# Cross attention with keys on the partitions: two heads a slot, no transposes of probabilities, values as one plain fp32 matmul

## The chip, the cores and the metric

One core of a Trainium2 chip runs the whole program. The metric is device time in microseconds, and the median of three runs is compared.

## The reference

One perceiver layer on x (256 tokens x 1024) with a context of 4096 tokens. Three sublayers, each behind a layer norm and added to x: cross attention, a decayed linear attention, and a mixture of low-rank experts. The change is in the first:

```python
q = (latents @ Wq).reshape(b, q_len, 4, 8, 128)           # 32 query heads, 4 key heads
k = (hidden_states @ Wk).reshape(b, kv_len, 4, 128)       # context and latents: 4352 rows
v = (hidden_states @ Wv).reshape(b, kv_len, 4, 128)
scores = jnp.einsum('bqhgd,bkhd->bhgqk', q, k) / sqrt(128)
attn = jax.nn.softmax(scores, axis=-1)
out = jnp.einsum('bhgqk,bkhd->bqhgd', attn, v)
return out.reshape(b, q_len, 4096) @ Wo
```

## The kernel before, in words

The program is a row of blocks, one after the other: keys and values (`project_keys_values`), attention (`cross_attention`), its output projection, the linear attention, its projection, the mixture. In each block the five engines run hand-written instruction lists, ordered by semaphores. SyncE (SP) issues all DMAs.

Precision: a matrix that goes through TensorE is split into a high part (rounded to fp32r, the format of TensorE's one-pass mode) and the rest, low. `three_pass` (L105 to L107) makes a product of three matmuls: high by high, high by low, low by high. Transposes run on plain fp32.

**Keys and values.** The context comes in eight chunks of 512 rows and one of the 256 latent rows. ScalarE copies the keys out of PSUM (`copy_keys`), VectorE the values, and both are stored in DRAM; the keys go there unsplit. The attention loads a key head in pieces and splits it again: ScalarE the high part (`act_piece`, L606), GpSimd the low (`pool_piece`, L682).

**Attention.** A slot serves one head; 32 slots, eight for each key head. Queries are on the partitions: scores of 128 queries x 512 keys, 18 units for a head (`pe_scores`), copied out by VectorE with the scale and a running maximum (`dve_scores`, L722). ScalarE exponentiates whole rows and sums them on the way (`act_exp`, L620). Probabilities are then transposed, two key tiles at a time, by TensorE (`pe_turn`, L822: four transposes of 128 x 128), split by ScalarE (L626) and VectorE (L747), and multiplied with the split values in three matmuls of 256 columns a key tile (`pe_values`). A step j of the slot does this for one pair of the 34 key tiles, so 17 steps; the scores of the next head, the query of the head after that (`pe_query`: 24 matmuls of 256 columns) and the inverse sums (`dve_inverse`, a diagonal spread by a matmul with ones, L853 and L854) are placed between. VectorE scales the output (L756) and SP stores it (L553).

Of the kernel before, what the change touches and what calls it, by code (L numbers as in the profile page):

```python
# [31 lines left out]
P = 128  # L32
# [52 lines left out]
class Shared:  # L85
# [3 lines left out]
    def __init__(self, a):  # L89
        self.r = [a.sb(f"split{i}", [P, KV], F32R) for i in range(2)]  # L90
        self.f = a.sb("full", [P, KV])
        self.stage = a.sb("stage", [P, 2 * PIECE])
        self.out = a.sb("head_out", [P, 2, TOK])


        self.last_keys = carve(self.f, 0, KVH, TOK)
        self.k_stored = a.sem("k_stored")
        self.v_stored = a.sem("v_stored")
        self.first_keys = [region[:, 0:FIRST * PIECE] for region in self.r]
        self.first_weight = [carve(region, FIRST * PIECE, KT, D) for region in self.r]  # L100
# [91 lines left out]
def project_keys_values(nc, x, ctxT, wk, wv, wq, x_sb, hT_hi, hT_lo, ident, kT_dram, v_dram, shared):  # L192
# [5 lines left out]
    with ExitStack() as ctx:  # L198
# [9 lines left out]
        k_out = a.sb("k_out", [P, KVH, CCHUNK])  # L208
# [17 lines left out]
        v_ready = a.sem("v_ready")  # L226
        k_copied = a.sem("k_copied")
# [4 lines left out]
        first_raw = (carve(shared.f, 0, KT, D), shared.f[:, KT * D:KT * D + FIRST * PIECE])  # L232
        first_split = list(zip(shared.first_weight, shared.first_keys))
# [8 lines left out]
        def store(sp, c, tiles, k_out):  # L242

            n = tiles * P
            sp.wait_ge(k_copied, KVH + KVH * (c + 1))
            sp.dma_start(kT_dram[:, :, bass.ds(c * CCHUNK, n)].rearrange("g p n -> p g n"),
                         k_out[:, :, 0:n]).then_inc(k_stored, 16)
            sp.wait_ge(v_copied, VT * (c + 1) + tiles)
            sp.dma_start(v_dram[:, :, bass.ds(c * VT, tiles), :].rearrange("g p t d -> p g t d"),
                         v_out[:, :, 0:tiles, :]).then_inc(v_stored, 16)  # L250

        @block.sync
        def _(sp):
            sp.sem_inc(k_stored, 16)
# [9 lines left out]
            sp.dma_start(x_sb[:, :, :], x).then_inc(x_in, 16)  # L264
            with sp.Fori(0, NCHUNK - 2) as c:
                sp.wait_ge(c_lo_ready, c + 1)
                load(sp, c + 2)
                store(sp, c, VT, k_out)
            store(sp, NCHUNK - 2, VT, k_out)
            sp.wait_ge(c_lo_ready, NCHUNK - 1)  # L270
            sp.dma_start(first_raw[0], wq[0]).then_inc(first_in, 16)
            sp.wait_ge(first_in, 16)
            sp.wait_ge(k_stored, 16 * NCHUNK)
            sp.dma_start(first_raw[1], kT_dram[0, :, 0:FIRST * PIECE]).then_inc(first_in, 16)
            store(sp, NCHUNK - 1, VT, k_out)
            store(sp, NCHUNK, QT, shared.last_keys)

        def copy_keys(act, c, n, k_out=k_out):

            for g in range(KVH):  # L280
                act.wait_ge(k_ready, KVH * c + g + 1)
                act.activation(k_out[:, g, 0:n], k_ps[:, g, 0:n], ACT.Copy).then_inc(k_copied, 1)
# [8 lines left out]
        def _(act):  # L291
            act.sem_inc(k_copied, KVH)
# [12 lines left out]
            with act.Fori(0, NCHUNK // 2 - 1) as i:  # L305
                for par in range(2):
                    c = 2 * i + 1 + par
                    next_hi(act, c, par)
                    act.wait_ge(k_stored, 16 * (c + 1))
                    copy_keys(act, c, CCHUNK)  # L310
            act.wait_ge(k_stored, 16 * NCHUNK)
# [3 lines left out]
            for i in range(2):  # L315
                act.wait_ge(first_in, 16 * (i + 1))
                act.activation(first_split[0][i], first_raw[i], ACT.Copy).then_inc(first_hi_ready, 1)
            act.wait_ge(first_lo_ready, 2)
            copy_keys(act, NCHUNK, TOK, shared.last_keys)

        @block.gpsimd
        def _(pool):
            for i in range(2):
                pool.wait_ge(first_hi_ready, i + 1)
                pool.tensor_tensor(first_split[1][i], first_raw[i], f32(first_split[0][i]),
                                   ALU.subtract).then_inc(first_lo_ready, 1)
# [14 lines left out]
        def _(dve):  # L341
            dve.sem_inc(v_copied, VT)
            for k in range(KT):
# [7 lines left out]
            split_low(dve, 1, 1)  # L351
            dve.wait_ge(x_in, 16)
# [7 lines left out]
            with dve.Fori(0, NCHUNK // 2 - 1) as i:  # L360
                for par in range(2):
                    c = 2 * i + 1 + par
                    split_low(dve, c + 1, par)
                    copy_values(dve, c, VT)
            ln.dve_lo(dve)
            copy_values(dve, NCHUNK - 1, VT)
# [23 lines left out]
        def _(pe):  # L390
# [22 lines left out]
            for t in range(QT):  # L413
# [7 lines left out]
PAIRS = KVT // 2  # L421
UNITS = [(qt, c0, min(BANK, KV - c0)) for qt in range(QT) for c0 in range(0, KV, BANK)]
NU = len(UNITS)
UPR = NU // QT
NS = 4
NPT = 3
LAG = 2
S_LAST = 11
DOUBLE = NU - 1 - S_LAST
UNITS_OF_STEP = [range(2 * j, 2 * j + 2) if j < DOUBLE else range(j + DOUBLE, j + DOUBLE + 1) if j <= S_LAST  # L430
                 else range(0) for j in range(PAIRS)]
Q_STEPS = range(S_LAST + 1, PAIRS - 1)


def piece_of(end):

    return (end - 1) // PIECE


def cross_attention(nc, wq, kT_dram, v_dram, hT_hi, hT_lo, ident, oT_dram, shared, proj):  # L440
# [9 lines left out]
    with ExitStack() as ctx:  # L450
        a = Alloc(nc, ctx, "xa_")
        v_hi = a.sb("v_hi", [P, KV], F32R)
        v_lo = a.sb("v_lo", [P, KV], F32R)
        kT_hi, kT_lo = shared.r
        rows = [[shared.f if (i, t) == (0, 0) else a.sb(f"rows{i}{t}", [P, KV]) for t in range(QT)] for i in range(2)]
        stage = [shared.stage[:, i * PIECE:(i + 1) * PIECE] for i in range(2)]
        w_raw = a.sb("w_raw", [P, KT, D])
        w_hi = a.sb("w_hi", [P, KT, D], F32R)
        w_lo = a.sb("w_lo", [P, KT, D], F32R)
        qT_hi = a.sb("qT_hi", [P, TOK], F32R)  # L460
        qT_lo = a.sb("qT_lo", [P, TOK], F32R)
        pT_hi = [a.sb(f"pT_hi{i}", [P, 2, TOK], F32R) for i in range(NPT)]
        pT_lo = [a.sb(f"pT_lo{i}", [P, 2, TOK], F32R) for i in range(NPT)]
        maxima = a.sb("maxima", [P, 2, QT, UPR])
        neg_max = a.sb("neg_max", [P, 2, QT])
        sums = a.sb("sums", [P, 2, QT, PIECES])
        total = a.sb("total", [P, QT])
        inverse = a.sb("inverse", [P, QT])
        ones = a.sb("ones", [P, P], F32R)
        diag_hi = a.sb("diag_hi", [P, TOK], F32R)  # L470
        diag_lo = a.sb("diag_lo", [P, TOK], F32R)
        scale_rows = a.sb("scale_rows", [P, TOK])
        o_out = [shared.out[:, i, :] for i in range(2)]
        s_ps = a.ps("s_ps", [P, NS, BANK])
        t_ps = a.ps("t_ps", [P, 2, 2, TOK])
        o_ps = a.ps("o_ps", [P, 2, TOK])
        m_ps = a.ps("m_ps", [P, 2, TOK])


        piece_asked = a.sem("piece_asked")  # L480
        piece_in = [a.sem(f"piece_in{i}") for i in range(2)]
        piece_hi = a.sem("piece_hi")
        piece_lo = a.sem("piece_lo")
# [3 lines left out]
        q_ready = a.sem("q_ready")  # L487
        q_hi_ready = a.sem("q_hi_ready")
        q_lo_ready = a.sem("q_lo_ready")
        s_ready = a.sem("s_ready")  # L490
        s_drained = a.sem("s_drained")
        max_ready = a.sem("max_ready")
        exp_done = a.sem("exp_done")
        turned = a.sem("turned")
        pT_hi_ready = a.sem("pT_hi_ready")
        pT_lo_ready = a.sem("pT_lo_ready")
        pv_done = a.sem("pv_done")
        sum_ready = a.sem("sum_ready")
        ones_set = a.sem("ones_set")
        diag_ready = a.sem("diag_ready")  # L500
        spread = a.sem("spread")
        spread_copied = a.sem("spread_copied")
        o_ready = a.sem("o_ready")
        o_stored = proj.stored
        block = ctx.enter_context(nc.Block())

        def slots(eng, kv_head_slot):

            def kv_head(g, last):
                for u in range(2):
                    kv_head_slot(eng, g, GROUP * g + u, u, last)
                with eng.Fori(1, GROUP // 2 - 1) as i:
                    for par in range(2):
                        kv_head_slot(eng, g, GROUP * g + 2 * i + par, 2 + par, last)
                for u in range(GROUP - 2, GROUP):
                    kv_head_slot(eng, g, GROUP * g + u, u, last)

            with eng.Fori(0, KVH - 1) as g:  # L520
                kv_head(g, False)
            kv_head(KVH - 1, True)

        def flags(u, last):

            return not (last and u == GROUP - 1), not (last and u >= GROUP - 2)

        def ahead(n, par, j):

            return (n, par, j + LAG) if j + LAG < PAIRS else (n + 1, 1 - par, j + LAG - PAIRS)  # L530

        def pt_free(n, j):

# [1154 lines left out]
```

## Time and profile before

| | |
|---|---|
| median of 3 runs | 2156.7 us (2156.37 to 2159.44) |
| profiled execution: its time, its span | 2159.04 us, 2157.2 us |
| TensorE matmuls, weight loads | 98%, 90% of the span |
| VectorE, ScalarE, GpSimd | 58%, 50%, 9% |
| DMA | mean 92 GB/s, 199.28 MB |
| granted TensorE clock | 0.994 |

Shares are busy time over the span. A busy TensorE isn't one at its peak, since its matmuls overlap and their ends are modelled; distances between starts say what one costs. In the rows PE is TensorE, PEld its weight loads, DVE VectorE, ACT ScalarE, POOL GpSimd, SP SyncE; L105 is line 105 of the kernel. Names that begin with xa_ are the attention's, kv_ the keys stage's, wo_ and lo_ the projections', la_ and pair_ the linear attention's; `full`, `split` and `stage` are buffers that the stages share.

### The profile page before, as it was taken

What the parts mean: (1) busy time and instruction counts of PE and PEld (TensorE: products, weight loads), DVE (VectorE), ACT (ScalarE), POOL (GpSimd) and SP (SyncE); (2) the same over time, 40 slices, a digit from 0 to 9 for tenths busy, and PEclk for the clock granted to TensorE, in tenths of its full rate; (3) what the DMA queues carried; (4) which work ended last, traced back from release to release, by engine and by line L of the source; (5) the groups of instructions that cost most, each with busy time, mean ns of one, the idle gap of its engine ahead of it and who ended that gap; (6) DMA issues with size and microseconds to landing.
All of it is one profiled execution on the core that took longest, in us unless ns stands there. A gap on an engine that the chain in (4) does not pass through costs nothing. (4 is left out here: it accounts for less than half of the span.)

```text
span 2157.2 us, 38230 instructions
## 1 busy us (share of the span) xinstructions
PE 2111.0 (98%) x14054; PEld 1937.6 (90%) x14054; DVE 1247.2 (58%) x2591; ACT 1070.2 (50%) x1604; POOL 192.2 (9%) x98
## 2 busy tenths in 40 slices
PE   8999999999999999999999999999999999999998
PEld 6888888799998999998999899998779999999886
DVE  5211110567676767766676767676574566666555
ACT  4111111566566656575666666566444544455442
POOL 0000001300012100031000310000000000000110
PEclk9999999999999999999999999999999999999999
DMA  6222212200012000120000210001745444455362
GB/s 234 102 113 97 78 69 80 82 26 13 24 45 78 14 26 12 46 75 27 14 25 30 76 41 13 26 12 55 274 148 209 181 175 175 179 189 191 133 233 79
DMA packets 57385, 199.28 MB, mean 92 GB/s; under 512 B 4592, under 2 KB 22000, under 8 KB 51760
## 3 DMA queue, kind: packets, MB, share of 16 engines
q1 hardware_dynamic: 57264, 197.71, 25.7%
q8 instruction: 71, 1.16, 0.2%
q14 instruction: 50, 0.41, 0.1%
HBM read 170.43 MB, written 27.26 MB: 92 GB/s over the span
## 5 line engine op out<-in xcount | busy, mean ns | idle before, releaser
L747 DVE TENSOR_TENSOR xa_pT_lo<-xa_t_ps,xa_pT_hi 128x512 fp32r<-128x512 f32 x544 | 372.6, 690 | 334.9 <-ACT xa_pT_hi L626 334.7
L626 ACT ACTIVATE xa_pT_hi<-xa_t_ps 128x512 fp32r<-128x512 f32 x544 | 321.8, 597 | 411.9 <-PE xa_t_ps L822 400.9
L105 PE MATMUL xa_o_ps<-xa_pT_hi,xa_v_hi 128*128 128x256 f32 x1088 | 310.1, 285 | 2.2 <-DVE xa_pT_lo L747 2.1
L107 PE MATMUL xa_o_ps<-xa_pT_hi,xa_v_lo 128*128 128x256 f32 x1088 | 308.5, 284 | 0.0
L106 PE MATMUL xa_o_ps<-xa_pT_lo,xa_v_hi 128*128 128x256 f32 x1088 | 307.9, 283 | 0.0
L822 PE MATMUL xa_t_ps<-ident,xa_rows 128*128 128x128 f32 x1632 | 294.8, 273 | 2.9 <-DVE xa_pT_lo L747 2.9
L722 DVE TENSOR_SCALAR_CACHE_REDUCE xa_rows<-xa_s_ps 128x512 f32<-128x512 f32 (+1 forms) x432 | 274.7, 652 | 0.2 <-PE xa_s_ps L107 0.2
L105 PE MATMUL xa_s_ps<-split,xa_qT_hi 128*128 128x512 f32 (+1 forms) x576 | 250.9, 436 | 0.9 <-DVE xa_qT_lo L716 0.9
L620 ACT ACTIVATE xa_rows<-xa_rows,xa_neg_max 128x1088 f32<-128x1088 f32 x192 | 229.6, 1196 | 0.0
L105 PEld LDWEIGHTS xa_o_ps<-xa_pT_hi,xa_v_hi 128*128 128x128 f32 x1088 | 207.2, 190 | 16.8 <-DVE xa_pT_lo L747 3.4
L107 PE MATMUL xa_s_ps<-split,xa_qT_lo 128*128 128x512 f32 (+1 forms) x576 | 220.8, 383 | 0.0
L106 PEld LDWEIGHTS xa_o_ps<-xa_pT_lo,xa_v_hi 128*128 128x128 f32 x1088 | 207.1, 190 | 13.8
L106 PE MATMUL xa_s_ps<-split,xa_qT_hi 128*128 128x512 f32 (+1 forms) x576 | 219.4, 381 | 0.0
L107 PEld LDWEIGHTS xa_o_ps<-xa_pT_hi,xa_v_lo 128*128 128x128 f32 x1088 | 207.4, 191 | 0.0
L822 PEld LDWEIGHTS xa_t_ps<-ident,xa_rows 128*128 128x128 f32 x1632 | 202.4, 141 | 4.0 <-issue 3.6
L1300 DVE TENSOR_TENSOR pair_lo<-pair_raw,pair_hi 128x4096 fp32r<-128x4096 f32 x30 | 132.8, 4425 | 81.2 <-ACT pair_hi L1237 81.2
L333 DVE COPY stage<-kv_v_ps 128x512 f32<-128x512 f32 x34 | 23.5, 691 | 243.2 <-PE kv_v_ps L107 243.2
L105 PE MATMUL la_qk_ps<-hT_hi,pair_hi 128*128 128x256 f32 x512 | 145.7, 285 | 2.8 <-PEq L928 2.8
L686 POOL TENSOR_TENSOR xa_w_lo<-xa_w_raw,xa_w_hi 128x1024 fp32r<-128x1024 f32 x31 | 74.5, 2403 | 798.4 <-ACT xa_w_hi L611 798.4
L107 PE MATMUL la_qk_ps<-hT_hi,pair_lo 128*128 128x256 f32 x512 | 145.6, 284 | 0.0
L106 PE MATMUL la_qk_ps<-hT_lo,pair_hi 128*128 128x256 f32 x512 | 145.6, 284 | 0.0
L822 PE MATMUL xa_t_ps<-ident,full 128*128 128x128 f32 x544 | 133.4, 274 | 6.1 <-DVE xa_pT_lo L747 6.1
(287 smaller groups left out, 4744.8 us busy)
## 6 DMA issues: line engine op xcount, KB each, us to landing
pair_raw<-in_w_qk SPq DMA_DIRECT2D x15, 2048.0 KB, 8.3
pair_raw<-in_w_gv SPq DMA_DIRECT2D x15, 2048.0 KB, 8.3
full<-in_wo SPq DMA_DIRECT2D x16, 1024.0 KB, 5.2
pair_raw<-in_w_out SPq DMA_DIRECT2D x16, 1024.0 KB, 5.1
xa_w_raw<-in_wq SPq DMA_DIRECT2D x31, 512.0 KB, 3.7
full<-in_ctxT SPq DMA_DIRECT2D x7, 2048.0 KB, 8.3
stage<-v_scratch SPq DMA_DIRECT2D x16, 544.0 KB, 3.8
kT_scratch<-kv_k_out SPq DMA_DIRECT2D x8, 1024.0 KB, 4.1
```

What stands on the lines that cost most here:

```text
L105: pe.matmul(out, w_hi, m_hi, start=first, stop=False)
L106: pe.matmul(out, w_hi, m_lo, start=False, stop=False)
L107: return pe.matmul(out, w_lo, m_hi, start=False, stop=last)
L333: dve.tensor_copy(v_out[:, :, t, :], v_ps[:, t, :].rearrange("p (g d) -> p g d", d=D)).then_inc(v_copied, 1)
L620: act.activation(row, row, ACT.Exp, bias=neg_max[:, par, qt:qt + 1], accum_out=sums[:, par, qt, e:e + 1]).then_inc(exp_done, 1)
L626: act.activation(pT_hi[j % NPT][:, :, :], t_ps[:, (par * PAIRS + j) % 2, :, :], ACT.Copy).then_inc(pT_hi_ready, 1)
L686: pool.tensor_tensor(w_lo[:, :, :], w_raw[:, :, :], f32(w_hi[:, :, :]), ALU.subtract).then_inc(w_lo_ready, 1)
L722: dve.tensor_scalar(rows[par][qt][:, c0:c0 + width], s_ps[:, (par * NU + k) % NS, 0:width], SCALE, None, ALU.mult, ALU.max, accum_out=maxi ...
L747: dve.tensor_tensor(pT_lo[j % NPT][:, :, :], t_ps[:, (par * PAIRS + j) % 2, :, :], f32(pT_hi[j % NPT][:, :, :]), ALU.subtract).then_inc(pT ...
L822: last = pe.transpose(t_ps[:, (par * PAIRS + j) % 2, t, qt * P:(qt + 1) * P], rows[par][qt][:, at], ident[:, :])
L1300: dve.tensor_tensor(w_lo[part][:, :, :], raw[part][:, :, :], f32(w_hi[part][:, :, :]), ALU.subtract).then_inc(w_lo_ready[part], 1)
```

## The change

- A slot serves two heads that share a key head: 16 slots. Keys are on the partitions, and both heads' queries (512) are the moving columns: a step j scores two key tiles into two banks of PSUM (`pe_scores`), and there are two such buffers.
- VectorE keeps an element-wise maximum over all key tiles (`dve_peak`) and ScalarE copies the scores out (`act_row`). At the slot's end the maximum is turned by four transposes (`pe_peak`), reduced (`dve_max`), put on a diagonal (`act_diag`) and spread over the partitions by a plain fp32 matmul with ones (`pe_spread`). In the next slot VectorE subtracts it (`dve_shift`) and ScalarE exponentiates (`act_exp`), step by step.
- The probabilities lie as the value matmul needs them: no transposes of them, no split. `pe_values` is one plain fp32 matmul of 512 columns a key tile.
- The sums are added by GpSimd (`pool_add`), spread by ones (`pe_sums`), inverted by four reciprocals of 128 columns (`dve_inverse`); ScalarE copies the output out (`act_output`), GpSimd scales it (`pool_output`). In the last slot VectorE takes half of the adds.
- Keys are split once, in the keys stage (ScalarE high, VectorE low: `copy_low_keys`), and stored in two parts, eight DMAs a chunk; values are stored whole. The attention loads both into place, in four pieces (`ENDS`), without another split. The query weight of two heads is loaded and split at once (2048 columns), and pe_query has 48 matmuls.

```diff
-                for qt in range(QT):
-                    last = pe.transpose(t_ps[:, (par * PAIRS + j) % 2, t, qt * P:(qt + 1) * P],
-                                        rows[par][qt][:, at], ident[:, :])
-            last.then_inc(turned, 1)
...
+        def pe_spread(pe, n, first=False):
+            pe.wait_ge(diag_ready, (W // P) * (n + 1))
+            if not first:
+                pe.wait_ge(shifted, J * n)
+            pe.matmul(r_ps[:, :], ones[:, :], diag[:, :], start=True, stop=True).then_inc(spread, 1)
...
+            pe.wait_ge(exp_done, J * n + j + 1)
             for t in range(2):
                 at = slice((2 * j + t) * P, (2 * j + t + 1) * P)
-                last = three_pass(pe, o_ps[:, par, :], v_hi[:, at], v_lo[:, at], pT_hi[j % NPT][:, t, :],
-                                  pT_lo[j % NPT][:, t, :], j == 0 and t == 0, j == PAIRS - 1 and t == 1)
+                last = pe.matmul(o_ps[:, :], v[:, at], probs[j % KEEP][:, t, :], start=j == 0 and t == 0,
+                                 stop=j == J - 1 and t == 1)
             last.then_inc(pv_done, 1)
...
+        def pe_slot(pe, n, u, g, first=False, last=False):
+            has_prev, has_next, has_query = flags(u, first, last)
+            par = u % 2
+            keys = g + 1 if u == 3 else None
+            values = g if u == 0 else None
+            if has_next:
+                pe_scores(pe, n + 1, 1 - par, (u + 1) % 2, 0, keys)
+            for j in range(J):
+                if has_next and j + 1 < J:
+                    pe_scores(pe, n + 1, 1 - par, (u + j) % 2, j + 1, keys)
+                pe_values(pe, n, j, values, not has_prev)
+                if has_prev and j == 2:
+                    pe_sums(pe, n - 1)
+            if has_next:
+                pe_peak(pe, n + 1)
+                if has_query:
+                    pe_query(pe, n + 3, 0, FILL)
+                pe_spread(pe, n + 1)
+                if has_query:
+                    pe_query(pe, n + 3, FILL, 2 * KT)
...
+        def pe_scores(pe, n, par, b, j, keys, first=False):
...
+            if not first or j >= 2:
+                pe.wait_ge(row_ready, J * n + j - 1)
             for t in range(2):
                 at = slice((2 * j + t) * P, (2 * j + t + 1) * P)
+                last = three_pass(pe, s_ps[:, 2 * b + t, :], kT_hi[:, at], kT_lo[:, at], qT_hi[:, par, :], qT_lo[:, par, :],
+                                  True, True)
+            last.then_inc(s_done, 1)
...
+        def act_row(act, n, b, j, first=False):
+            act.wait_ge(peak_done, J * n + j + 1)
+            if not first:
+                act.wait_ge(exp_done, J * (n - 1) + j + 1)
+            act.activation(rows[j], s_ps[:, 2 * b:2 * b + 2, :], ACT.Copy).then_inc(row_ready, 1)
...
+            for j in range(J):
+                if j + 1 < J:
+                    act_exp(act, n, j + 1, not has_prev, not has_next)
+                if has_next:
+                    act_row(act, n + 1, (u + 1 + j) % 2, j)
+                if has_next and has_query and j == 2:
+                    act_query(act, n + 2, u % 2)
...
+                if has_query and j == 4:
+                    act_weight(act, n + 3)
...
+            if j < J - 2:
+                dve.tensor_tensor(peak[:, :, :], s_ps[:, 2 * b:2 * b + 2, :], peak[:, :, :], ALU.max).then_inc(peak_done, 1)
+                if j == J - 3:
+                    dve.wait_ge(peak_done, J * n + j + 1)
+                    dve.tensor_tensor(peak[:, 0, :], peak[:, 0, :], peak[:, 1, :], ALU.max).then_inc(peak_part, 1)
+                return
...
+        def dve_shift(dve, n, j):
+            dve.wait_ge(row_ready, J * n + j + 1)
+            dve.wait_ge(spread, n + 1)
+            dve.tensor_tensor(rows[j], rows[j], r_ps[:, :].unsqueeze(1).to_broadcast([P, 2, W]), ALU.subtract).then_inc(shifted, 1)
...
+            for j in range(J):
                 if has_next:
+                    dve_peak(dve, n + 1, (u + 1 + j) % 2, j)
+                if j + 1 < J:
+                    dve_shift(dve, n, j + 1)
...
+                if has_prev and 4 <= j < 8:
+                    dve_inverse(dve, n - 1, j - 4)
...
+                pool.wait_ge(added, (J - 1) * n + j - 1)
+                pool.tensor_tensor(sums[:, :, :], sums[:, :, :], probs[j % KEEP], ALU.add).then_inc(added, 1)
...
+            for g in range(KVH):
+                dve.wait_ge(k_hi_ready, KVH * c + g + 1)
+                dve.tensor_tensor(k_lo[:, g % 2, 0:n], k_ps[:, g, 0:n], f32(k_hi[:, g % 2, 0:n]),
+                                  ALU.subtract).then_inc(k_copied, 1)
```

`W` is 512, `J` 17, `KEEP` 3 (probability buffers), `FILL` 12, `PAIRS` 16 now counts pairs of heads. `flags` gives has_prev (not the first slot), has_next (not the last) and has_query (not the last three); GpSimd's `pool_slot` does an add a step, the weight's low part at j = 6 and `pool_output` at j = 9.

## Rows read from the trace of the kernel before

**Rows 1.** Windows: stretch, its length, then busy us (count) of each engine, clock, DMA share, GB/s.
```profile
0.00:385.40 385.40, 375.16 (x1696) 312.34 (x1696) 78.26 (x89) 68.79 (x77) 10.68 (x10) 1.00 0.30 108
385.40:1519.60 1134.20, 1116.55 (x8000) 1044.46 (x8001) 783.95 (x2019) 704.76 (x1185) 147.87 (x60) 0.99 0.11 36
```

**Rows 2.** Waits in the attention stage: engine, waiting tile <- releaser: total us, times, longest.
```profile
ACT xa_pT_hi L626 <- PE xa_t_ps L822: 400.9, 341, 2.7
...
PE xa_t_ps L822 <- DVE xa_pT_lo L747: 9.0, 7, 2.0
```

**Rows 3.** Timeline of TensorE, transposes and value matmuls: start us, us, instruction.
```profile
902.88 0.27 PE L822 MATMUL xa_t_ps<-ident,full 128*128 128x128 f32 x1
902.99 0.27 PE L822 MATMUL xa_t_ps<-ident,xa_rows 128*128 128x128 f32 x1
...
904.82 0.28 PE L106 MATMUL xa_o_ps<-xa_pT_lo,xa_v_hi 128*128 128x256 f32 x1
904.94 0.28 PE L107 MATMUL xa_o_ps<-xa_pT_hi,xa_v_lo 128*128 128x256 f32 x1
```

**Rows 4.** Timeline, handing over between engines, and two VectorE operations in a row.
```profile
390.52 0.42 DVE L716 TENSOR_TENSOR xa_qT_lo<-xa_m_ps,xa_qT_hi 128x256 fp32r<-128x256 f32 x1 [6.37 <-ACT xa_qT_hi L615]
391.00 0.50 PE L105 MATMUL xa_s_ps<-split,xa_qT_hi 128*128 128x512 f32 x1 [0.93 <-DVE xa_qT_lo L716]
...
391.57 0.39 PE L107 MATMUL xa_s_ps<-split,xa_qT_lo 128*128 128x512 f32 x1
391.80 0.40 PE L105 MATMUL xa_s_ps<-split,xa_qT_hi 128*128 128x512 f32 x1
...
392.10 0.69 DVE L722 TENSOR_SCALAR_CACHE_REDUCE full<-xa_s_ps 128x512 f32<-128x512 f32 x1 [1.16 <-PE xa_s_ps L107]
...
901.25 1.29 DVE L747 TENSOR_TENSOR xa_pT_lo<-xa_t_ps,xa_pT_hi 128x512 fp32r<-128x512 f32 x2 [0.53 <-ACT xa_pT_hi L626]
```

**Rows 5.** Timeline of SP's queue: the output stores of two consecutive heads.
```profile
831.80 0.35 SPq L553 DMA_DIRECT2D oT_scratch<-head_out  x1
...
866.34 0.35 SPq L553 DMA_DIRECT2D oT_scratch<-head_out  x1
```

**Rows 6.** Line 1059, four plain fp32 matmuls of one column: ns min/median/max, first, last start.
```profile
L1059 PEld LDWEIGHTS lo_turned<-ones,square_sum x8: 187/192/195, 2036.8 to 2037.6; 128*128 128x128 f32 x8
L1059 PE MATMUL lo_turned<-ones,square_sum x8: 242/250/253, 2036.8 to 2037.6; 128*128 128x1 f32 x8
```

**Rows 7.** Groups by form: busy us, mean ns of one | idle before it.
```profile
L747 DVE TENSOR_TENSOR xa_pT_lo<-xa_t_ps,xa_pT_hi 128x512 fp32r<-128x512 f32 x544 | 372.6, 690 | 334.9 <-ACT xa_pT_hi L626 334.7
L626 ACT ACTIVATE xa_pT_hi<-xa_t_ps 128x512 fp32r<-128x512 f32 x544 | 321.8, 597 | 411.9 <-PE xa_t_ps L822 400.9
...
L620 ACT ACTIVATE xa_rows<-xa_rows,xa_neg_max 128x1088 f32<-128x1088 f32 x192 | 229.6, 1196 | 0.0
...
L1300 DVE TENSOR_TENSOR pair_lo<-pair_raw,pair_hi 128x4096 fp32r<-128x4096 f32 x30 | 132.8, 4425 | 81.2 <-ACT pair_hi L1237 81.2
...
L1237 ACT ACTIVATE pair_hi<-pair_raw 128x4096 fp32r<-128x4096 f32 x30 | 108.2, 3608 | 0.0
...
L611 ACT ACTIVATE xa_w_hi<-xa_w_raw 128x1024 fp32r<-128x1024 f32 x31 | 32.6, 1050 | 0.1
```

**Rows 8.** Groups by form: VectorE's reciprocals of two columns and of one.
```profile
L734 DVE RECIPROCAL xa_inverse<-xa_total 128x2 f32<-128x2 f32 x32 | 5.3, 166 | 1.1
...
L153 DVE RECIPROCAL lo_ln_r<-lo_ln_root 128x1 f32<-128x1 f32 x2 | 0.3, 154 | 0.3 <-ACT lo_ln_root L169 0.3
```

**Rows 9.** Line 686, GpSimd's subtraction of 1024 columns: ns min/median/max.
```profile
L686 POOL TENSOR_TENSOR xa_w_lo<-xa_w_raw,xa_w_hi x31: 2394/2406/2408, 395.0 to 1440.5; 128x1024 fp32r<-128x1024 f32 x31
```

**Rows 10.** Timeline of TensorE after a wait near the stage's start.
```profile
408.67 0.33 PE L822 MATMUL xa_t_ps<-ident,full 128*128 128x128 f32 x1 [1.99 <-DVE xa_pT_lo L747]
...
410.08 0.63 PE L105 MATMUL xa_s_ps<-split,xa_qT_hi 128*128 128x512 f32 x1
410.50 0.63 PE L106 MATMUL xa_s_ps<-split,xa_qT_hi 128*128 128x512 f32 x1
```

More of the change, by code:

```diff
@@ L253, in _ @@
         def _(sp):
-            sp.sem_inc(k_stored, 16)
+            for par in range(2):
+                sp.sem_inc(k_stored[par], 32)
             sp.sem_inc(v_stored, 16)
@@ L440, in cross_attention, with piece_of, starts_piece @@
-def cross_attention(nc, wq, kT_dram, v_dram, hT_hi, hT_lo, ident, oT_dram, shared, proj):
+FILL = 12
+KEEP = 3
+def piece_of(j):
+    return next(i for i, end in enumerate(ENDS) if j < end)
+def starts_piece(j):
+    return j == 0 or j in ENDS
+def cross_attention(nc, wq, k_drams, v_dram, hT_hi, hT_lo, ident, ones, oT_dram, shared, proj):
     with ExitStack() as ctx:
         a = Alloc(nc, ctx, "xa_")
-        v_hi = a.sb("v_hi", [P, KV], F32R)
-        v_lo = a.sb("v_lo", [P, KV], F32R)
         kT_hi, kT_lo = shared.r
[L455 to L483, printed above, removed]
@@ new lines, in act_exp @@
+        def act_exp(act, n, j, first=False, last=False):
+            act.wait_ge(shifted, J * n + j + 1)
+            back = j - KEEP
+            if back >= 0:
+                act.wait_ge(pv_done, J * n + back + 1)
+                if not last:
+                    act.wait_ge(added, (J - 1) * n + max(back, 1))
+                elif back >= 2 and back % 2 == 0:
+                    act.wait_ge(added_last, back // 2)
+                else:
+                    act.wait_ge(added, (J - 1) * n + (back + 2) // 2)
+            elif not first:
+                before = max(x for x in range(J) if x % KEEP == j)
+                act.wait_ge(pv_done, J * (n - 1) + before + 1)
+                act.wait_ge(added, (J - 1) * (n - 1) + before)
+            act.activation(probs[j % KEEP], rows[j], ACT.Exp, scale=SCALE).then_inc(exp_done, 1)
@@ new lines, in pe_sums, with pe_sums_last @@
+        def pe_sums(pe, n):
+            pe.wait_ge(sum_ready, n + 1)
+            pe.wait_ge(max_ready, n + 2)
+            pe.matmul(t_ps[:, :], ones[:, :], sum_row[:, :], start=True, stop=True).then_inc(sum_spread, 1)
+        def pe_sums_last(pe):
+            pe.wait_ge(inverse_ready, 4 * LAST + 4)
+            pe.wait_ge(added, (J - 1) * LAST + J // 2)
+            pe.wait_ge(added_last, J // 2)
+            pieces = [part[:, t, :] for part in (sums, peak) for t in range(2)]
+            for i, part in enumerate(pieces):
+                last = pe.matmul(t_ps[:, :], ones[:, :], part, start=i == 0, stop=i == len(pieces) - 1)
+            last.then_inc(sum_spread, 1)
```

710 lines of the change are left out of this document (343 added, 367 removed).

## The prediction

> **What bounds the kernel now.** I read the windows by stage first, then who waited for whom in the attention stage, then TensorE's timeline inside it. The attention stage lies from 385.4 to 1519.6 us: 1134.2 us, 53% of the span, and TensorE is busy in 1116.6 of them, VectorE in 784, ScalarE in 705, GpSimd in 148 [rows 1]. TensorE's longest waits there are below 10 us a line; the large ones are those of ScalarE and VectorE for TensorE's transposes [rows 2]. So the stage costs what TensorE's instructions cost back to back. Busy times overstate that, since matmuls overlap, so I take distances between starts: a transpose of 128 columns every 0.11 us, a value matmul of 256 every 0.12 [rows 3], a score matmul of 512 every 0.23 [rows 4]. One head by these prices: scores 3 x (16 x 0.23 + 2 x 0.12) = 11.8, values 34 x 3 x 0.12 = 12.2, transposes 68 x 0.11 = 7.5, query 24 x 0.12 = 2.9, spreading the inverse sums 0.2: 34.6 us. The stores of two consecutive heads are 34.54 us apart [rows 5]. The price list holds; a pair of heads costs 69.2.
>
> **TensorE after the change.** One slot now serves two heads. Scores: 34 key tiles x 3 x 0.23, that is 1.38 a step of two tiles. The 136 transposes (15.0) go; four of the maximum (0.44) come. Query as before, 48 x 0.12 = 5.8. Values: one plain fp32 matmul of 512 columns for each key tile, in place of six of 256 (0.72 for both heads). No row shows a wide one. The only plain fp32 matmuls that aren't transposes are four of one column, and they left eight loads and eight matmuls in the trace [rows 6]: two records each. Below: each record streams the 512 columns once, 2 x 0.23 = 0.46. Above: the moving operand is taken in two parts as well, so four terms (the three of the helper, and low by low), 4 x 0.23 = 0.92, and both loads stand bare, 2 x 0.11 more: 1.14. A load is otherwise hidden: value matmuls of 256 columns run at 0.12 with a load each [rows 3]. I take 0.92, because a full product of an operand in two parts needs both parts of the other: 1.84 a step. (The Trainium skill, "FP8 and Floating Point Precision", TensorE Precision Notes, counts four passes for true FP32; no run so far shows it. By it the value step would be the same 1.84, by the lower bound 0.92.) The two matmuls by ones, for the maximum and for the sums, are plain fp32 too, 0.92 each. A slot: 17 x (1.38 + 1.84) + 5.8 + 0.4 + 1.8 = 62.8 us, 6.4 below 69.2. So what the transposes give (15.0) goes to half into dearer values (31.3 against 24.5).
>
> **The chain in a slot.** Each step's scores S(j) of the next pair go to two PSUM banks. VectorE takes the maximum (dve_peak j) and shifts the present pair's rows (dve_shift j+1), ScalarE exponentiates those, and only then copies the scores out (act_row j); S(j+2) waits for that copy. From the end of S(j)'s issue: 0.30 to VectorE's start (a unit's last matmul issued at 391.57, the next one at 391.80, VectorE at 392.10) [rows 4]; maximum of 1024 columns 1.22 (690 ns for 512, 4425 for 4096, so 1.04 ns a column) [rows 7]; shift 1.13, since two in a row take 0.09 less than twice one [rows 4]; 0.06 from engine to engine, as from VectorE's end at 390.94 to TensorE at 391.00 [rows 4]; Exp 1.10 (1196 ns for 1088 columns with an accumulator, a copy of 1024 in 1050) [rows 7]; row copy 0.97 (597 ns for 512, 3608 for 4096, less some overlap) [rows 7]; 0.06 to TensorE. Together 4.84. TensorE has V, S, V to do meanwhile: 5.06. So 0.22 is spare in a step of 3.22, of which VectorE is busy 2.35 and ScalarE 2.07. That is tight, and what comes on top shows:
> - At the slot's start S(0) and S(1) stand together, so only S(1) and V(0), 3.22, cover the 4.84: a stall of 1.6.
> - Step 14 has one more maximum over 512 columns, 0.75 with its wait: stall 0.5.
> - The weight's high part is now 2048 columns on ScalarE, 1.9 (twice 1050 ns less the fixed part); ScalarE has 1.15 free in a step: 0.75 late, stall 0.5.
> - Four reciprocals of 128 columns. The rows have 154 ns for one column and 166 for two [rows 8], so between one column's 1.04 ns (0.29 in all) and 12 ns a column (1.7). I take 1.1, 7 ns a column, the middle of the slope: VectorE has 0.87 free in a step, each runs late by 0.15, 0.3 in all after the slack. (The Trainium skill, "VectorE: DVE Perf Modes", First, the fixed hardware budget, has a reciprocal repeat its divide eight times; no run so far shows a wide one. By it the four would be near the 1.1 I use; by one cycle a column they'd be 0.29, and their stall goes.)
>
> The slot's end costs nothing while a query follows: VectorE's reduction 0.7 and four diagonals on ScalarE of some 0.3 each lie inside 36 query matmuls (4.3). GpSimd's sixteen adds of 1024 columns take 2.41 each [rows 9], less than a step; the weight's low part (4.7), a product and a sum (1.3 each) make it 46 us of a slot, and three probability buffers let it lag by 5. Key loads have a whole slot of cover, at a DMA share of 0.11 [rows 1]. Slot: 62.8 + 1.6 + 0.5 + 0.5 + 0.3 = 65.7.
>
> **The stage.** Thirteen slots with a query: 854. Two without query and weight: 62.8 - 5.8 + 2.2 (the wait between transposes and spread lies bare) + 2.4 = 61.6 each, 123. The last: 2.7 until its first Exp is there, 17 x 1.84 = 31.3, four matmuls by ones 3.7, four bare reciprocals 4.4, product and handing over 1.7: 44. The start: query 5.8, and 1.6 more if the clock is low as in [rows 10]; splitting 1.5; thirteen score steps at 2.0 (two buffers, handed back after 2.6), four with query work at 2.8, 6.7 for weight and query work that waits on ScalarE and GpSimd, then 8.8 to the first slot: 62. Sum 62 + 854 + 123 + 44 = 1083 against 1134.2: 51 less.
>
> **The keys stage.** VectorE gets 36 more subtractions of 0.69, ScalarE's copies stay, and SP issues eight key stores a chunk where it was one. VectorE is busy 78 of 385 us there [rows 1] and the subtractions end while TensorE is on the values, so nothing moves; without that cover it would be 25. The first keys need no splitting any more; GpSimd's split of the first weight (4.7) has a chunk of cover. The stages behind keep their work. The profiled execution took 2159.0, its span 2157.2, the median of the runs is 2156.7: 51 off the median gives **2105 us**.
>
> **The rivals.**
> - *Dearer values, slower than before.* If plain fp32 loads aren't hidden, the value step is 2.28 and the slot 71.4 (the chain then has slack, only 1.2 of stall stays), 5.7 more; with the last slots 96 us more, **2201**. For it: the loads in the trace stood 0.11 apart with nothing wide over them [rows 6]. Against: all wide matmuls hide theirs. It decides from 1.03 us a tile matmul, 3.7 us a slot.
> - *Fewer stalls or cheaper values.* Without any stall 43 less, **2062**. At 0.46 a value matmul the chain sets the step, (1.38 + 4.84)/2 = 3.11, and all stalls stay: **2065**. Cheap values bring little.
> - *The clock falls in the stalls.* After 1.99 us idle between transposes, matmuls of 512 columns came 0.42 apart, 1.2 GHz, for some 3.3 us [rows 10]. Fifteen slot starts at 1.6 lost: 24 more, **2129**. Against: 2.8 us of matmuls stand before this stall.
> - *Longer handoffs.* Each 0.1 in the chain beyond the slack costs 0.05 a step, 14 us in 272 steps; 0.5 more is 33 us after the slack, **2138**. It reaches no change at 0.9.
> - *GpSimd's adds set the pace.* That needs 3.6 us an add. At 4.0 its slot is 16 x 4.0 + 7.3 = 71.3, 5.6 more in fifteen slots: **2189**. Against: its subtractions beside VectorE keep to 2394 to 2408 ns [rows 9].
>
> **Chances.** The forecast (2085 to 2130) 0.47; fewer stalls or cheaper values 0.16; clock 0.12; handoffs 0.10; dearer values 0.11; GpSimd 0.04. A measurement here can tell 0.2% from no change. Faster: the first three and 0.09 of the handoffs, 0.84; within 0.2% 0.02; slower 0.14. The range runs from the floor without stalls, 2062, past the longer handoffs to 2165; it leaves out dearer values and GpSimd.
>
> **What would show it.** Value matmuls in two records each, two tiles 1.84 apart; no transposes but four a slot; stores of pairs 65.7 apart; TensorE waiting for ScalarE's row copy at the third score step of a slot, 1.6 us, and 0.5 near steps 7 and 16; GpSimd's adds at 2.4; reciprocals near 1.1; VectorE busy some 70% of the stage, ScalarE 60%. The prediction is wrong if tile matmuls stand over 1.0 apart, if the step is over 3.4, or if GpSimd's adds pass 3.6.

## The result, and the profile after

The changed kernel takes 2127.3 us in the median against 2156.5 for the kernel before, measured beside it: ratio 0.9856, 95% interval 0.9837 to 0.9875. The forecast was 2105, in a range of 2062 to 2165. So the change is a gain of 29 us, where 51 were forecast. The profiled execution took 2128.1 us, its span 2126.3. One of the four executions of the changed kernel took 7100.9 us; the ratio leaves it out, and without it the median is 2126.6.

The windows of the changed kernel, by stage (length, then busy us and count of TensorE, its loads, VectorE, ScalarE and GpSimd, clock, DMA share, GB/s):

```profile
0.00:383.90 383.90, 374.10 (x1696) 311.54 (x1697) 101.10 (x125) 66.67 (x76) 5.46 (x8) 1.00 0.37 134
383.90:1482.50 1098.60, 1006.43 (x3622) 622.83 (x3622) 770.64 (x700) 603.93 (x658) 697.92 (x293) 0.98 0.13 44
1482.50:2126.30 643.80, 624.01 (x4358) 584.80 (x4358) 386.05 (x483) 296.70 (x343) 34.56 (x28) 0.98 0.50 182
```

Against [rows 1] the attention stage went from 1134.2 to 1098.6 us, 35.6 less. TensorE's busy time in it fell by 110 us (1116.6 to 1006.4), and its time not busy rose from 18 to 92 us. GpSimd's 148 became 698. The keys stage is 1.5 us shorter. What lies behind the attention stage is 643.8 us, where the spans of before leave 2157.2 - 1519.6 = 637.6: 6.2 longer. -35.6 - 1.5 + 6.2 = -30.9, the difference of the two spans.

Who TensorE waited for in the attention stage of the changed kernel (us in total, times, longest):

```profile
PE xa_s_ps L111 <- ACT xa_rows L608: 42.6, 32, 2.5
PE xa_s_ps L111 <- ACT full L608: 23.7, 17, 1.5
PE xa_o_ps L878 <- ACT stage L632: 5.4, 3, 2.6
PE xa_q_ps L111 <- POOL xa_w_lo L677: 4.7, 1, 4.7
```

In [rows 2] the other engines waited for TensorE's transposes. Now TensorE waits 66 us for ScalarE's row copy (L608; `xa_rows` and `full` are both buffers of rows), the last link of the chain that the prediction priced. The stores of pairs that follow each other, from SP's timeline:

```profile
813.90 0.41 SPq L553 DMA_DIRECT2D oT_scratch<-head_out  x1
881.14 0.41 SPq L553 DMA_DIRECT2D oT_scratch<-head_out  x1
946.73 0.41 SPq L553 DMA_DIRECT2D oT_scratch<-head_out  x1
1013.99 0.41 SPq L553 DMA_DIRECT2D oT_scratch<-head_out  x1
```

They are 67.24, 65.59 and 67.26 us apart, where one head took 34.54 [rows 5], two 69.1. A step of scores and values on TensorE's timeline:

```profile
883.33 1.88 PE L878 MATMUL xa_o_ps<-xa_probs,xa_v 128*128 128x512 f32 x4
884.91 0.52 PE L111 MATMUL xa_s_ps<-xa_qT_hi,split 128*128 128x512 f32 x1
...
886.43 1.02 PE L878 MATMUL xa_o_ps<-stage,xa_v 128*128 128x512 f32 x2
```

From one value step to the next is 3.10 us, and scores take 1.38 of it, so the four records of a value step (two tiles, two records each) take 1.72: 0.43 a record, 0.86 a wide plain fp32 matmul. Eight value records in a row, from 898.47 to 901.90, give the same 0.43.

Where a slot loses time, TensorE's timeline of one slot shows in three places:

```profile
915.01 0.50 PE L111 MATMUL xa_s_ps<-xa_qT_hi,split 128*128 128x512 f32 x1 [1.45 <-ACT full L608]
...
931.91 0.50 PE L111 MATMUL xa_s_ps<-xa_qT_hi,split 128*128 128x512 f32 x1 [0.26 <-ACT xa_rows L608]
...
958.23 1.88 PE L878 MATMUL xa_o_ps<-xa_probs,xa_v 128*128 128x512 f32 x4
962.59 0.50 PE L111 MATMUL xa_s_ps<-xa_qT_hi,split 128*128 128x512 f32 x1 [2.48 <-ACT xa_rows L608]
...
963.62 0.59 PE L112 MATMUL xa_s_ps<-xa_qT_lo,split 128*128 128x512 f32 x1
964.01 0.63 PE L113 MATMUL xa_s_ps<-xa_qT_hi,split 128*128 128x512 f32 x1
964.43 4.91 PE L878 MATMUL xa_o_ps<-stage,xa_v 128*128 128x512 f32 x8
```

The third score step, the weight's step and step 16: the forecast had 1.6, 0.5 and 0.5. The last is 2.48. The idle time in brackets counts from a modelled end. By starts the loss is larger: 962.59 - 958.23 - 1.72 = 2.64, and the first matmul after it takes 0.33 instead of 0.23. So the three cost 1.71, 0.53 and 2.75, together 4.99 us a slot. In seven slots of twelve, this one among them, the clock falls behind the long wait: the last score matmuls are 0.42 apart, 1.2 GHz, and eight value records take 4.75 instead of 3.44 (granted clock 0.72 over the 6.2 us from the wait's end, 1.00 in the other five). Such a slot is 1.6 us longer, which is the difference between 67.2 and 65.6.

Why step 16's scores come late is on the other engines' timeline:

```profile
956.39 2.38 POOL L688 TENSOR_TENSOR xa_sums<-xa_sums,xa_probs 128x1024 f32<-128x1024 f32 x1
956.59 2.74 DVE L749 TENSOR_TENSOR xa_peak<-xa_peak 128x512 f32<-128x512 f32 x1
...
959.25 1.21 DVE L765 TENSOR_TENSOR xa_rows<-xa_rows,xa_r_ps 128x1024 f32<-128x1024 f32 x1
960.38 0.68 DVE L753 TENSOR_TENSOR xa_peak<-xa_s_ps,xa_peak 128x512 f32<-128x512 f32 x1
960.57 1.06 ACT L632 ACTIVATE stage<-xa_rows 128x1024 f32<-128x1024 f32 x1 [3.90 <-DVE xa_rows L765]
961.09 0.69 DVE L755 TENSOR_TENSOR xa_peak<-xa_s_ps,xa_peak 128x512 f32<-128x512 f32 x1
961.53 1.01 ACT L608 ACTIVATE xa_rows<-xa_s_ps 128x1024 f32<-128x1024 f32 x1
```

The maximum of the two halves of `peak` (L749) is recorded at 2.74 us. The two operations of the same size that read a PSUM bank (L753, L755) take 0.69. GpSimd's add began 0.2 us earlier and ended at 958.77; the merge ends at 959.33, 0.56 later. It looks as if it stood until the add was over. Over the whole run its durations spread widely (ns, min/median/max), and the shortest is the one merge that stands before GpSimd's first add:

```profile
L749 DVE TENSOR_TENSOR xa_peak<-xa_peak x16: 691/2700/2782, 433.5 to 1418.6; 128x512 f32<-128x512 f32 x16
```

The Trainium skill, "SBUF — State Buffer", SBUF: two separate sides, gives the rule: VectorE and GpSimd share a port pair that is locked, not divided; a VectorE operation with two SBUF inputs needs it against a GpSimd operation that reads SBUF, and the one that starts first holds it for its whole instruction. This trace fits it. The other fifteen merges are recorded at 2.09 to 2.78 us, depending on how far the add had come, and every one of them ends 0.54 to 0.56 us after the add does. The experiments below test it.

### The profile page after: what moved, and what is told of

The parts are those of the page before. It is cut to its first block and busy times, and to the rows that moved or that the text cites. A ratio compares the mean times of both kernels' runs of the same rounds, so it can differ in the third digit from the quotient of the medians.

```text
span 2126.3 us, 26815 instructions
## 1 busy us (share of the span) xinstructions
PE 2004.5 (94%) x9676; PEld 1519.2 (71%) x9676; DVE 1257.8 (59%) x1308; ACT 967.3 (45%) x1077; POOL 737.9 (35%) x329
## 5 line engine op out<-in xcount | busy, mean ns | idle before, releaser
L688 POOL TENSOR_TENSOR xa_sums<-xa_sums,stage 128x1024 f32<-128x1024 f32 x150 | 357.6, 2384 | 103.3 <-ACT stage L632 98.5
L878 PE MATMUL xa_o_ps<-stage,xa_v 128*128 128x512 f32 x768 | 369.6, 608 | 5.4 <-ACT stage L632 5.4
L746 DVE TENSOR_TENSOR xa_peak<-xa_s_ps,xa_peak 128x1024 f32<-128x1024 f32 x224 | 272.8, 1218 | 147.1 <-PE xa_s_ps L113 147.0
L111 PE MATMUL xa_s_ps<-xa_qT_hi,split 128*128 128x512 f32 x544 | 262.7, 483 | 69.9 <-ACT xa_rows L608 42.6
L765 DVE TENSOR_TENSOR xa_rows<-xa_rows,xa_r_ps 128x1024 f32<-128x1024 f32 x208 | 251.1, 1208 | 0.0
L111 PEld LDWEIGHTS xa_s_ps<-xa_qT_hi,split 128*128 128x128 f32 x544 | 102.5, 188 | 200.2 <-ACT xa_rows L608 132.8
L632 ACT ACTIVATE stage<-xa_rows 128x1024 f32<-128x1024 f32 x144 | 152.3, 1057 | 164.3 <-DVE xa_rows L765 163.7
L608 ACT ACTIVATE xa_rows<-xa_s_ps 128x1024 f32<-128x1024 f32 x208 | 209.8, 1009 | 36.0 <-DVE xa_peak L746 19.1
L113 PE MATMUL xa_s_ps<-xa_qT_hi,split 128*128 128x512 f32 x544 | 216.5, 398 | 0.0
L112 PE MATMUL xa_s_ps<-xa_qT_lo,split 128*128 128x512 f32 x544 | 215.2, 396 | 0.0
L688 POOL TENSOR_TENSOR xa_sums<-xa_sums,xa_probs 128x1024 f32<-128x1024 f32 x75 | 179.3, 2390 | 31.8 <-ACT xa_probs L632 27.3
L113 PEld LDWEIGHTS xa_s_ps<-xa_qT_hi,split 128*128 128x128 f32 x544 | 103.1, 190 | 23.6
```

Of the source, the lines that this page charges most:

```text
L111: pe.matmul(out, w_hi, m_hi, start=first, stop=False)
L112: pe.matmul(out, w_hi, m_lo, start=False, stop=False)
L113: return pe.matmul(out, w_lo, m_hi, start=False, stop=last)
L608: act.activation(rows[j], s_ps[:, 2 * b:2 * b + 2, :], ACT.Copy).then_inc(row_ready, 1)
L632: act.activation(probs[j % KEEP], rows[j], ACT.Exp, scale=SCALE).then_inc(exp_done, 1)
L688: pool.tensor_tensor(sums[:, :, :], sums[:, :, :], probs[j % KEEP], ALU.add).then_inc(added, 1)
```

## The experiments

The theory: TensorE's own work is a slot of about 61 us, and everything above it is the lateness of one chain (peak, shift, exponential, row copy), made worse in step 14 by the blocked merge. The rivals: TensorE's values bind, or GpSimd's adds set the pace. Each median is compared with the kernel before, measured in turn with it.

**Row copy first.** In every step of `act_slot`:

```diff
-                if j + 1 < J:
-                    act_exp(act, n, j + 1, not has_prev, not has_next)
                 if has_next:
                     act_row(act, n + 1, (u + 1 + j) % 2, j)
+                if j + 1 < J:
+                    act_exp(act, n, j + 1, not has_prev, not has_next)
```

> The edit: in every step of a slot ScalarE copies the scores of the next pair out of PSUM before it takes the exponential, not behind it. Nothing is left out. Theory (stalls come from one chain: peak 1.22 us, shift 1.21, exponential 1.06, row copy 1.01, plus handoffs, 4.68 us between a score step and the release of the one after next): the shift and the exponential leave the chain, which becomes about 0.3 + 1.22 + 1.01 + 0.1 = 2.6 us. The waits of 1.45, 0.26 and 2.48 us in each slot go, and with them the half clock that follows the 2.48 us one in every second slot (0.8 us per slot on the mean), so a slot is 66.87 - 4.2 - 0.8 = 61.9 us, and the kernel 2127 - 15 x 4.7 = about 2060 us. The addition on VectorE at step 14 still takes 2.7 us. Rival (TensorE's own work fills the slot, value matmuls dearer than thought): the waits move elsewhere and the time stays within 10 us of 2127. Rival (GpSimd's 16 adds of 2.39 us and the merge that they block set the end of a slot): the wait near step 14 stays over 2 us and only the 1.45 goes: about 2105 us.

Measured: 2045.7 us, ratio 0.9478 (0.9463 to 0.9494), 82 us below the changed kernel. Its stage and two consecutive stores:

```profile
384.70:1403.20 1018.50, 985.13 (x3622) 626.57 (x3622) 745.51 (x700) 630.17 (x658) 702.55 (x293) 0.99 0.14 47
```

```profile
603.46 0.42 SPq L553 DMA_DIRECT2D oT_scratch<-head_out  x1
664.04 0.41 SPq L553 DMA_DIRECT2D oT_scratch<-head_out  x1
```

A slot is 60.6 us, and none of the three waits is left in it. This is TensorE's floor: 60.6 + 4.99 = 65.6, the shorter slot of the changed kernel. Both rivals fall. I expected 2060; most of the miss is that by starts the three waits cost 4.99 us a slot, where I had taken off the 4.2 recorded as idle. One detail was expected otherwise: in twelve of the sixteen slots the merge takes 0.83 to 0.86 us.

```profile
854.11 2.38 POOL L688 TENSOR_TENSOR xa_sums<-xa_sums,stage 128x1024 f32<-128x1024 f32 x1
856.19 0.85 DVE L749 TENSOR_TENSOR xa_peak<-xa_peak 128x512 f32<-128x512 f32 x1
856.57 2.72 POOL L688 TENSOR_TENSOR xa_sums<-xa_sums,xa_probs 128x1024 f32<-128x1024 f32 x1
```

Here the merge starts 0.30 us before the end of one add (856.49) and ends 0.55 us after it, at 857.04. The next add starts while the merge runs, and it takes 0.34 us more than its usual 2.38. The one that comes second pays, in either direction. In this run too all fifteen merges that meet an add end 0.54 to 0.56 us after it: they don't run slower beside it, they stand until it is over. What the row order changed is when the merge comes, late in an add and not at its beginning.

**Merge with one SBUF input.** The diagonal's tile is free at that time and takes the result; steps 15 and 16 and the transposes use it too:

```diff
-                    dve.tensor_tensor(peak[:, 0, :], peak[:, 0, :], peak[:, 1, :], ALU.max)
+                    dve.tensor_reduce(diag[:, :], peak[:, :, :].rearrange("p t n -> p n t"), AX.X, ALU.max)
```

> The edit: at step 14 the two halves of the running maximum are merged by a reduction with a single SBUF input into another tile (that of the diagonal, free at that time) where an elementwise maximum with two SBUF inputs stood; the last two steps work on that tile. Nothing is left out. Theory (the merge of 0.69 us takes 2.74 us because it has two SBUF inputs and waits for GpSimd's add of 2.38 us to end): the reduction is about 1.2 us long in every slot, whatever GpSimd does, so the wait of 2.48 us falls to about 0.9 us, the half clock after it goes too; slot 66.87 - 1.5 - 0.8 = 64.5 us, kernel about 2092 us. Rival (the merge is slow because of its own operands or because VectorE has to wait for memory in any form): the reduction is 2.7 us or more and the time stays at 2127 or rises. Rival (the 2.48 us wait is ScalarE's own lateness): the merge is shorter, the wait stays over 2 us, 2127 us.

Measured: 2095.7 us, ratio 0.9712 (0.9695 to 0.9728), 32 us below. The reduction beside a running add, and its spread over the run:

```profile
814.99 2.39 POOL L688 TENSOR_TENSOR xa_sums<-xa_sums,xa_probs 128x1024 f32<-128x1024 f32 x1
815.15 1.25 DVE L749 TENSOR_REDUCE xa_diag<-xa_peak 128x512 f32<-128x1024 f32 x1
```

```profile
L749 DVE TENSOR_REDUCE xa_diag<-xa_peak x16: 1252/1258/1287, 434.9 to 1390.6; 128x512 f32<-128x1024 f32 x16
```

It reads the same 1024 values of a partition as the merge, but as one input, starts 0.16 us into the add, and isn't delayed. The wait at step 16 falls to 0.99 us, slots are 64.1 us apart. The running maximum of the changed kernel (L746), the merge's own operation with one input in PSUM and one in SBUF, keeps to 1.23 us beside an add as well (949.13, beside the add of 949.00). So it isn't VectorE's work beside GpSimd that is slow, but the form with two SBUF inputs.

**Small adds.** GpSimd's adds of steps 3 to 16 on 8 columns of each half:

```diff
-                pool.tensor_tensor(sums[:, :, :], sums[:, :, :], probs[j % KEEP], ALU.add)
+                pool.tensor_tensor(sums[:, :, 0:8], sums[:, :, 0:8], probs[j % KEEP][:, :, 0:8], ALU.add)
```

> The edit: GpSimd's additions of the probabilities in steps 3 to 16 take 16 of 1024 columns; their number, order and semaphores stay. Left out: most of the sum of the probabilities, so the output is not the reference's. Theory (the add blocks the merge with two SBUF inputs): an add is some tenths of a us, the merge of step 14 is back at 0.7 us as in the kernel before, the wait of 2.48 us falls to about 0.5 us, the forecast's value; slot about 64 us, in the last slot VectorE's adds are 1.2 us and not 1.83; kernel about 2085 to 2092 us. The wait of 1.45 us at the start of a slot stays. Rival (the merge is slow by itself): merge 2.7 us, wait 2.4 us, 2127 us. Rival (GpSimd's adds set the pace of a slot through the release of the probability buffers): all three waits go, about 2060 us.

Measured: 2083.8 us, ratio 0.9659 (0.9642 to 0.9675). The untouched merge:

```profile
L749 DVE TENSOR_TENSOR xa_peak<-xa_peak x16: 691/692/695, 433.8 to 1380.1; 128x512 f32<-128x512 f32 x16
```

Without the long adds it is 0.69 us all sixteen times, and the wait at step 16 is 0.44, close to the 0.5 forecast. The wait at the slot's start stays at 1.45: GpSimd doesn't set it. This settles the cause of the large wait: the same instruction is 2.7 us beside an add and 0.69 without one.

**Both edits,** row copy first and the merge with one SBUF input.

> The edits of the two kernels with the row copy ahead of the exponential and with the merge of a single SBUF input together. Nothing is left out. Theory: the first edit already takes the merge off the path but for some 0.2 us (2.48 less the 2.27 us of shift and exponential), so both together are 2 to 5 us below the first alone: about 2057 us. Rival (the merge still sets a wait of its own when ScalarE's order is right): 20 us or more below the first alone.

Measured: 2046.3 us, ratio 0.9485 (0.9469 to 0.9501), the same as the row order alone (0.9478). I expected 2 to 5 us less; none shows. With the row order right the merge has cover.

**Half the values.** One matmul of each value step is left out:

```diff
-            for t in range(2):
-                at = slice((2 * j + t) * P, (2 * j + t + 1) * P)
-                last = pe.matmul(o_ps[:, :], v[:, at], probs[j % KEEP][:, t, :], start=j == 0 and t == 0,
-                                 stop=j == J - 1 and t == 1)
+            at = slice(2 * j * P, (2 * j + 1) * P)
+            last = pe.matmul(o_ps[:, :], v[:, at], probs[j % KEEP][:, 0, :], start=j == 0, stop=j == J - 1)
```

> The edit: of each value step only the first of its two matmuls is issued, on the changed kernel with its order on ScalarE as it is. Left out: half of the value product, so the output is not the reference's. Theory (a score buffer comes free 4.68 us after its step's last matmul is issued, and the score step itself is 1.38 us, so two steps can't take less than 6.06 us, where TensorE now needs 6.20): of 0.86 us taken from each of 16 steps only 0.07 comes back in the steps with scores, and the full 0.86 in the last one or two of a slot, some 2 to 3 us of a slot of 66.9; kernel about 2085 to 2105 us. Rival (TensorE's own work sets the steps): 16 x 0.86 x 16 pairs = 220 us come back, 1907 us.

Measured: 2098.5 us, ratio 0.9736 (0.9712 to 0.9760), 29 us below the changed kernel for 220 us of matmuls left out. TensorE's timeline:

```profile
804.18 0.50 PE L111 MATMUL xa_s_ps<-xa_qT_hi,split 128*128 128x512 f32 x1 [0.55 <-ACT xa_rows L608]
807.30 0.50 PE L111 MATMUL xa_s_ps<-xa_qT_hi,split 128*128 128x512 f32 x1 [0.60 <-ACT xa_rows L608]
810.36 0.50 PE L111 MATMUL xa_s_ps<-xa_qT_hi,split 128*128 128x512 f32 x1 [0.55 <-ACT xa_rows L608]
```

Two steps take 6.18 us, against 6.20 with all values. The chain (4.68) and the score step (1.38) make 6.06 of it; behind a wait the first score matmul takes 0.34 us and not 0.23, and the sum is 6.17. So in the changed kernel the chain leaves 0.14 us of slack in two steps, of which 0.02 is left once TensorE waits, and any lateness becomes a wait.

**Half the values with the row copy first.**

> The edit: only the first of the two matmuls of each value step, on the kernel with the row copy ahead of the exponential. Left out: half of the value product. Theory (with that order TensorE bounds the slot, its floor 60.6 us as measured): the cut now pays until the next engine binds, VectorE with 1.22 + 1.21 = 2.43 us a step, so 3.10 falls towards 2.45 us a step and a slot from 60.8 to about 50 to 52 us: 1905 to 1925 us, and TensorE has waits in every step. Rival (something other than TensorE, the handoffs or GpSimd, already bounds the slot with that order): no more than 45 us below 2045.

Measured: 1938.7 us, ratio 0.8985 (0.8965 to 0.9005), 107 us below the row order alone; slots are 53.3 us apart. With that order TensorE's work does bind, and less of it pays: 7.3 of the 14.6 us left out of a slot come back. It stops 14 us above the top of what I expected. TensorE now waits most for ScalarE's exponentials:

```profile
PE xa_o_ps L877 <- ACT stage L632: 45.1, 36, 2.7
PE xa_s_ps L111 <- ACT xa_rows L608: 35.7, 48, 1.5
```

**Row copy first in a slot's first step alone,** j = 0.

> The edit: the row copy ahead of the exponential in the first step of a slot alone. Nothing is left out. Theory (each wait is a delay of its own, worth its idle time and about 0.25 us of a late first matmul and drained pipe): the wait at the third score step of a slot goes (1.71 us with the drain), the 2.48 us one near the end stays with its half clock: 15 x 1.7 = 26 us less, about 2102 us. Rival (the wait only moves to the next score step, whose buffer is as late): unchanged within 5 us of 2127.

Measured: 2109.9 us, ratio 0.9785 (0.9766 to 0.9805), 17 us below the changed kernel and not 26. The rival is half right: the 1.45 goes, but the next score step waits 0.60 (the second row; the first is step 16's wait, unchanged).

```profile
823.47 0.50 PE L111 MATMUL xa_s_ps<-xa_qT_hi,split 128*128 128x512 f32 x1 [2.49 <-ACT xa_rows L608]
845.42 0.50 PE L111 MATMUL xa_s_ps<-xa_qT_hi,split 128*128 128x512 f32 x1 [0.60 <-ACT full L608]
```

In a chain without slack a wait taken away at one place comes back in part at the next. The clock differs too: in this run's profile it falls behind two of the twelve long waits of 2.44 to 2.50 us, where in the changed kernel's it falls behind seven of twelve. No run shows what decides it.

**The ends of the stage,** on the kernel with the row copy first:

```diff
             act_query(act, 0, 0)
+            act_weight(act, 1)
             for j in range(J):
                 act_row(act, 0, j % 2, j, True)
-                if j == 2:
-                    act_weight(act, 1)
...
-                if not has_next and j == 11:
+                if not has_next and j == J - 1:
                     proj.low(dve, 0, 0)
```

> The edit: the kernel with the row copy ahead of the exponential, and two moves outside the slots with both scores and values: the first query weight is split right behind the first query instead of behind three row copies, and VectorE's split for the output projection stands behind its last shift and not four steps before the end of the last slot. Nothing is left out. Theory: TensorE's wait of 4.7 us for the weight's low part near the start of the stage goes (GpSimd's 4.5 us starts some 8.5 us earlier), and the wait of 2.6 us in the last slot with the waits around it goes; together 6 to 9 us below the row order alone, about 2038 us. Rival (both are covered by a later wait, for the chain of score buffers at the start and for the last reciprocals at the end): within 2 us of 2045.7.

Measured: 2037.9 us, ratio 0.9452 (0.9431 to 0.9473), the fastest version here. The stage is 1008.5 us against 1018.5 in the profiles. TensorE's wait of 4.7 us for the weight and the one of 2.59 us late in the last slot are gone; the 2.56 us at that slot's start and 1.38 in it stay. What stays is 5.01 us before the output projection, behind the last four reciprocals, and then the half clock (granted 0.50):

```profile
1392.79 0.77 PE L111 MATMUL wo_y_ps<-split 128*128 128x512 f32 x1 [5.01 <-PEq L466]
1393.35 0.63 PE L112 MATMUL wo_y_ps<-split 128*128 128x512 f32 x1
```

## Why the prediction held, and where it was off

The likeliest case was right in its mechanism: transposes gone, TensorE's floor a little lower, a chain through two score buffers that is as long as TensorE's work. The gain was 22 us smaller than forecast. That it still fell into the likeliest band is in part luck: in the slots a stall dearer by 39 us stands against values cheaper by 28. By pieces of the profiled run:

| piece | forecast | measured |
|---|---|---|
| start to the first slot | 62 | 61.05 (383.90 to 444.95) |
| 13 slots with a query | 854 | 865.55 (to 1310.50) |
| two slots without | 123 | 121.6 (to 1432.1) |
| last slot | 44 | 50.5 (to 1482.56) |
| keys stage | 0 | -1.5 |
| behind the stage | 0 | +6.2 |

- **The stall at step 14 is the term that was mis-sized most:** "0.75 with its wait: stall 0.5". Measured 2.75 us with the late first matmul, and 0.8 on average for the half clock behind it, because the merge took 2.7 us, not 0.69. That is 3 us in 13 slots, 39 us. In the rows that I read of before, VectorE's operations in this stage have a PSUM input (L722, L747) [rows 4, 7]; the change brought one a slot with two SBUF inputs and, with it, adds that fill GpSimd. I priced the adds, but not what they do to VectorE. The rival on GpSimd looked only at its own pace, which was right: its adds stayed at 2.38 us.
- **Value matmuls:** two records each, as forecast; 0.86 us, not 0.92. A step is 3.10, not 3.22, and the floor of a slot 60.6 us (measured with the row copy first), not 62.8. That gives 28 us back in 13 slots and hides most of the miss above. The four passes that the Trainium skill ("FP8 and Floating Point Precision", TensorE Precision Notes) counts come, as an estimate, to 0.92 at the 0.23 of the score matmuls; the trace has 0.86, near to it and far from the lower bound of 0.46.
- **The chain:** forecast 4.84, measured 4.68 (issue of S(0)'s last matmul over at 910.33, S(2) at 915.01), with TensorE's cover down from 5.06 to 4.82. That is 0.14 us of slack in two steps, and by the half-values run 0.02 once TensorE waits, where the forecast had 0.22. The slot start's stall was 1.71 for 1.6, the weight's 0.53 for 0.5.
- **Reciprocals:** 0.95 us for 128 columns, not 1.1, and no wait behind them.
- **The clock:** I had it fall at slot starts. There it doesn't (1.00 in the 8 us behind each of the twelve waits of 1.45 to 1.53 us); it does after seven of the twelve waits of 2.4 to 2.5 us. The rival's mechanism exists, in another place.
- **The last slot** was 6.5 us too cheap: I took its sixteen value steps back to back, but the projection's split (L975, 4.5 us for two beside GpSimd's adds, 2.36 alone) holds VectorE's shifts up, TensorE waits 2.6 us, and 1.4 and 0.3 before it, and the first eight records take 5.1 us, where eight take 3.6 elsewhere (granted clock 0.72).
- **Behind the stage:** the projection starts after 5.01 us of idle at 1.2 GHz, which makes its 97.5 us 98.9. Most of the rest lies in the last block: from its first load to the output's store 133.9 us in the kernel before, 138.6 in the changed one, 139.4 with the row copy first and 136.3 with the ends moved. No edit touches that block, and TensorE's clock in it accounts for about all of the 4.7 us between the first two. The mixture's first 24 matmuls stand 0.21 us apart in the changed kernel (granted clock 0.50 from 2104.60 to 2110.50) and 0.12 in the kernel before (1.00 from 2138.40 to 2142.00), which puts the next instruction 2.3 us later. The projection's matmuls take 1.6 us more, with a granted clock of 0.65 behind a wait of 2.45 us where it was 1.00 behind one of 1.35, and the last stretch to the store 0.9 more, at 0.53 against 0.75. I had put nothing down for these stages. Why the clock comes out lower there stays open.
- **The rival of longer handoffs** has a slip: by its own price of 14 us for each 0.1 beyond the slack, the gain of 51 us is gone at about 0.6 more in the chain, not at 0.9.
- **Busy shares:** VectorE 70% of the stage, as forecast; ScalarE 55%, not 60.

## What to carry to other kernels

When work goes from one engine to another, look for what the new work locks and not only for how long it is: list every VectorE operation with two SBUF inputs that will run beside GpSimd, and price it as if it began when the GpSimd operation ends. On an in-order engine, put the operation that hands a buffer back ahead of the one that only feeds the next step: swapping two lines of ScalarE's order gave 82 us here, nearly three times what the whole change had given. And when a chain and the bounding engine come out within a few per cent, take the difference as zero and add up the stalls; but of one stall removed by itself expect only a part back (here 0.86 of 1.71 us a slot).

## What the runs showed of the hardware

- A VectorE maximum of 512 columns with two SBUF inputs took 0.69 us without GpSimd's long adds (all sixteen, 691 to 695 ns) and up to 2.78 us when it began during one; in the changed kernel and with the row copy first, all thirty that did so ended 0.54 to 0.56 us after the add. A reduction with one SBUF input took 1.25 to 1.29 us beside the same adds. An add that began during the maximum took 2.72 us in place of 2.38.
- A wide plain fp32 matmul (128 by 512) is two load and matmul records, 0.43 us apart, its loads hidden: 0.86 us.
- A reciprocal of 128 columns out of PSUM takes 0.95 us; with the 154 ns of one column [rows 8] that is 6.2 ns a column.
- A wait of TensorE behind plain fp32 matmuls cost about 0.25 us more than the idle time in the record: 0.16 by the distance of starts and 0.1 of a slower first matmul.
- The clock stayed at 2.4 GHz (granted 1.00) behind all twelve waits of 1.45 to 1.53 us at slot starts. Behind waits of 2.4 to 2.5 us it fell to 1.2 GHz in seven of twelve in the changed kernel and in two of twelve with the first row copy moved, and that cost 1.6 us each time in the changed kernel.
